# Sums over two chunks of exponentials added beforehand on VectorE, for two head pairs of each later batch

## The reference

```python
# first layer, per batch: 16 heads of 64, 256 tokens, 512 context rows
q = (lat @ Wq);  k, v = split(ctx @ Wkv);  k = apply_rope(k, cos, sin)
attn = clip(q @ k.T * scale, -11, 11)
attn = softmax(attn, axis=-1)
x = x + (attn @ v) @ Wo + bo
# second layer, per token: attention among 16 heads of width 8, then 8 experts
kv = (h @ Wdown + bdown) @ Wup + bup
x = x + out_proj;  x = x + sum_e gate_e * (h2 @ We[e])
```

## Time and profile before

| | |
|---|---|
| time, median of 3 runs | 317.58 us (317.51 to 318.62) |
| the profiled execution's own time | 318.85 us |
| its span, first to last instruction | 317.0 us |
| TensorE busy | 295.0 us (93%) |
| VectorE busy | 241.6 us (76%) |
| GpSimd busy | 208.6 us (66%) |
| ScalarE busy | 164.0 us (52%) |

### The profile page before, as it was taken

One profiled execution on the slowest core, in us unless ns is written; L12 is line 12 of the kernel. 1 busy time (PEld: TensorE's weight loads), 2 busy tenths in 40 slices (PEclk: granted clock), 3 DMA queues, 4 the chain that ended last, 5 costly groups with the idle time before them and its releaser, 6 DMA issues.

```text
span 317.0 us, 6676 instructions
## 1 busy us (share of the span) xinstructions
PE 295.0 (93%) x2514; PEld 206.9 (65%) x2514; DVE 241.6 (76%) x448; ACT 164.0 (52%) x326; POOL 208.6 (66%) x207
## 2 busy tenths in 40 slices
PE   6888999999999999998999999999999999899983
PEld 6776576666668766665777676566786665486651
DVE  2985997675884849899888788977647699687856
ACT  2446456667443735573425555874426468404741
POOL 5445875765572839786645777498927588868764
PEclk9999999999999999999999999999999999999998
DMA  7563412111210111111111112011101100000001
GB/s 207 169 160 90 134 44 68 52 35 46 58 26 9 38 31 35 36 33 33 35 35 33 28 27 50 13 40 37 32 19 33 47 7 2 0 19 0 3 0 33
DMA packets 16319, 14.24 MB, mean 45 GB/s; under 512 B 4832, under 2 KB 11808, under 8 KB 16288
## 3 DMA queue, kind: packets, MB, share of 16 engines
q1 hardware_dynamic: 14992, 13.49, 16.2%
q10 hardware_dynamic: 1296, 0.33, 0.5%
HBM read 4.89 MB, written 0.52 MB: 17 GB/s over the span
## 4 chain that ended last, share of the span: by engine, by line
PE 54%; DVE 20%; issue 7%; POOL 5%; ACT 5%; DMA 4%; SPq 3%; POOLq 0%; ACTq 0%; DVEq 0%
PE pv L631 12%; PE sc L617 10%; PE sums L652 7%; PE side L738 4%; PE pj_k L555 3%; SPq L522 3%; DVE ks L1262 3%; PE side L814 2%; PE pj_k L557 2%; PE pj_k L556 2%; DMA kswap<-ksin 2%; DMA sin_in<-in_L_xattn_sin_dram 2%; DVE ksin L1326 2%; ACT e L926 2%; POOL e L1768 1%
## 5 line engine op out<-in xcount | busy, mean ns | idle before, releaser
L1768 POOL TENSOR_SCALAR e<-e 128x1024 f32<-128x1024 f32 x64 | 71.6, 1118 | 64.2 <-ACT e L926 56.8
L926 ACT ACTIVATE e<-sc 128x1024 f32<-128x1024 f32 x64 | 65.6, 1025 | 31.3 <-PE sc L617 31.2
L617 PEld LDWEIGHTS sc<-qs,ks 64*128 64x128 f32 x768 | 49.6, 185 | 25.9 <-issue 24.0
L617 PE MATMUL sc<-qs,ks 64*128 64x256 f32 x768 | 62.5, 294 | 2.3 <-ACT e L926 2.2
L631 PE MATMUL pv<-e,v 128*64 128x256 f32 x512 | 62.3, 385 | 1.6 <-POOL e L1768 1.1
L1761 POOL TENSOR_TENSOR krot<-kcos,kswap 128x512 f32<-128x512 f32 x32 | 45.7, 1429 | 9.4 <-DMA kswap<-ksin 7.6
L631 PEld LDWEIGHTS pv<-e,v 128*64 128x64 f32 x512 | 34.1, 136 | 24.0 <-issue 6.8
L934 ACT ACTIVATE u<-pv 128x256 f32<-128x256 f32 x32 | 12.4, 386 | 61.6 <-PE pv L631 61.6
L1262 DVE TENSOR_TENSOR ks<-krot,ks 128x512 fp32r<-128x512 f32 x32 | 32.4, 1012 | 0.1
L1326 DVE TENSOR_TENSOR ksin<-pj_k,sinT 128x512 f32<-128x512 f32 x32 | 21.9, 685 | 3.8 <-PE pj_k L557 3.5
L918 ACT ACTIVATE v<-pj_k 128x512 f32<-128x512 f32 x28 | 16.5, 600 | 13.9 <-PE pj_k L557 13.5
(11 more groups left out here) (293 smaller groups left out, 578.1 us busy)
## 6 DMA issues: line engine op xcount, KB each, us to landing
kswap<-ksin SPq DMA_DIRECT2D x126, 64.0 KB, 2.0
ctx_in<-in_ctx_dram SPq DMA_DIRECT2D x4, 256.0 KB, 3.5
prod<-in_L_xattn_Wkv_dram SPq DMA_DIRECT2D x2, 512.0 KB, 6.3
x_in<-in_x_dram SPq DMA_DIRECT2D x1, 512.0 KB, 6.4
prod<-in_L_xattn_Wq_dram SPq DMA_DIRECT2D x1, 512.0 KB, 7.2
wo<-in_L_xattn_Wo_dram SPq DMA_DIRECT2D x1, 512.0 KB, 4.4
fwe<-in_L_ffn_We_dram SPq DMA_DIRECT2D x1, 512.0 KB, 4.4
out_dram<-x_in SPq DMA_DIRECT2D x3, 128.0 KB, 1.8
```

The source lines that it names most:

```text
L617: last = nc.tensor.matmul(sc[:, h, c * NT:(c + 1) * NT], ks[rows, j % 3, k_part, chunk], qs[rows, j % 2, q_part, :], start=(k_part + q_par ...
L926: nc.scalar.activation(e[:, j % 3, :, 2 * half:2 * half + 2, :].rearrange("p h c n -> p h (c n)"), sc[:, :, :], ACT.Exp, scale=SCALE).then ...
L1768: nc.gpsimd.tensor_scalar(a, a, EXP_HIGH, EXP_LOW, ALU.min, ALU.max).then_inc(s_clip, 1)
```

## The change

`chunks_added(j)` holds for the first batch as before, and now for pairs 2 and 3 of each later batch (pairs 10, 11, 18, 19, 26, 27). For these VectorE runs `add_chunks` twice a pair, in the slot after the pair's own (slots 11 and 12, 19 and 20, 27 and 28), right behind `key_lo` and ahead of the "mid" pieces. The results go to `e_added_later`, which lies in the buffer `on`. `sums(11)`, `sums(19)` and `sums(27)` use 8 matmuls in place of 16 (the profile records each as two), and wait for the additions. They move within slots 12, 20 and 28, from ahead of `times_values` to the end of the slot, behind side step "b" and the `values` unit. In the first batch, and for the other pairs, nothing changes.

```diff
+def chunks_added(j):
+    return j < PAIRS or j % PAIRS in (2, 3)
...
+        e_added_later = on.rearrange("p k n -> p (k n)").rearrange("p (j c h n) -> p j c h n", j=2, c=2, h=2)
...
+        def added_of(pair):
+            return e_added if pair < PAIRS else e_added_later
...
 # TensorE, sums(j)
-                if j < PAIRS:
+                if chunks_added(j):
                     n = 2
-                    pe.wait_ge(s_added, 2 * j + 2)
+                    pe.wait_ge(s_added, 2 * sum(chunks_added(i) for i in range(j + 1)))
...
 # TensorE, the loop over slots
-                if 2 <= slot <= NPAIR and slot % 2 == 0:
+                late = slot > PAIRS and chunks_added(slot - 1)
+                if 2 <= slot <= NPAIR and slot % 2 == 0 and not late:
                     sums(slot - 1)
                 if 1 <= slot <= NPAIR:
                     times_values(slot - 1)
...
                 for n in value_units(slot):
                     values(n)
+                if slot % 2 == 0 and late:
+                    sums(slot - 1)
...
 # VectorE, add_chunks(j, half)
-                nc.vector.tensor_tensor(e_added[:, j % 2, half, :, :], e[:, j % 3, :, 2 * half, :],
+                nc.vector.tensor_tensor(added_of(j)[:, j % 2, half, :, :], e[:, j % 3, :, 2 * half, :],
                                         e[:, j % 3, :, 2 * half + 1, :], ALU.add).then_inc(s_added, 1)
...
 # VectorE, the loop over slots
                     key_lo(slot + 1)
+                if slot > PAIRS and chunks_added(slot - 1):
+                    add_chunks(slot - 1, 0)
+                    add_chunks(slot - 1, 1)
                 second_layer(slot, "mid")
```

More of the change, by code:

```diff
@@ L652, in sums @@
                         last = nc.tensor.matmul(sum_bank[32 * g:32 * g + 32, 0:NT], w,
-                                                e_added[:, pair % 2, c, g % 2, :] if j < PAIRS
+                                                added_of(pair)[:, pair % 2, c, g % 2, :] if chunks_added(j)
                                                 else e[:, pair % 3, g % 2, c, :],
```

## The result

The changed kernel takes 322.64 us (median of 4 runs, 321.65 to 324.38) against 317.54 us for the kernel before on the same chip: ratio 1.014, interval 1.0108 to 1.0172. It is slower, by more than the range of the prediction allowed. A later repetition gave 1.0134 (1.0075 to 1.0194), a difference of 3.9 us between the medians where this one has 5.1.

What follows compares the result with a forecast made beforehand. The prediction took TensorE's instruction list, busy 93% of the span, as the bound. Its places summed to -1.4 + 1.9 + 0.5 = +1.0 us on the 317.58 us median: 318.6 us, +0.3%, range 315.4 to 321.4.

Steps and rivals of the forecast that it cites:

- waiting GpSimd work going behind both additions: Slots 11, 19, 27: GpSimd's waiting clip starts only after both VectorE additions, delaying the release by 1.2 us in slots 20, 28.
- The first rival: VectorE and GpSimd swap the shared SBUF access after each addition; sum +3.6 us, 321.2 us, slower; chance 0.27.
- likeliest case: GpSimd waits behind both additions: -1.4 (slot 12), +1.9 (slot 20), +0.5 (slot 28), 318.6 us; chance 0.50.
- The saving: Three calls of `sums` on TensorE go from 1.86 to 1.00 us: 0.86 us each, 2.6 us in all.
- The wait for `recS`: TensorE's 0.93 us wait at the start of slot 17, expected to shrink by 0.54 to about 0.4 us.
- The root: GpSimd's inverse root in slot 19, behind the clip, expected 1.2 us later, moving the release in slot 20 equally.
- the uncovered release: VectorE's bank release for `keyval2`: in slot 20 1.0 us after TensorE's earlier arrival, in slot 28 0.34 us ahead, without push.
- VectorE is never late: Rival: VectorE's idle quarter absorbs the additions in all slots, leaving only -2.6 us, 314.1 to 315.0 us; chance 0.10.
- The access costs nothing: Rival: shared SBUF access delays no GpSimd work here; -1.8 + 0.7 - 0.7 = -1.8, 315.8 us; chance 0.13.

Runs made afterwards that it cites:

- the run with the PSUM operand: Changed kernel with the second operand of the twelve new additions read from PSUM instead of SBUF: 317.61 us, ratio 0.9971 to the kernel before.
- the middle batch alone: Changed kernel with the change kept only for pairs 18 and 19 (slots 19 and 20): 320.73 us, ratio 1.0068 to the kernel before.
- the filled waits: Changed kernel plus matmuls that serve nothing where TensorE would wait, in slots 12, 20 and 28: 322.12 us, ratio 1.0095 to the kernel before.
- the move alone: Changed kernel without the twelve new additions; sums of slots 12, 20, 28 moved but over four chunks: 320.06 us, ratio 1.0051 to the kernel before.
- the early form of all three places: Changed kernel; pairs 10, 18, 26, 19 added in own slots, `sums(19)` at its old place, `query_down` additions before context split: 316.13 us, ratio 0.9922 to kernel before.
- the own-slot version: Changed kernel with additions of pairs 10, 18, 26 made late in their own slots: 318.95 us, ratio 1.0008 to the kernel before.

## Why the prediction was wrong

One mechanism was taken the wrong way round, one term was not in the sum at all, and some smaller ones were mis-sized.

**The step that failed** is "waiting GpSimd work going behind both additions". The first rival holds: the access changes hands after each instruction. What I had named as its sign, an addition of over 0.7 us, is there in five of the six pairs (in slot 11 both), and the run with the PSUM operand shows that it goes away with the second SBUF operand, their number and place unchanged. The prediction even had the clue in hand: it took the 1.32 us of the clip in slot 19 to mean that the clip had stood waiting behind the key split, and then let it begin behind two additions that come only after that split. I had followed one undisturbed pair against two rows beside it that spoke for the rival. It is also the only pair of the first batch whose additions stand back to back; in the other seven the second waits for a clip, which is the 12.1 us of the earlier trace rows. Why that pair, with a rotation waiting since 43.64, kept the access stays open. It is no accident: the pair takes 1.28 us and that rotation 2.34 in all thirteen traces, while the six new pairs went by the order of asking.

**By places**, likeliest case, rival, and measured:

| | likeliest | rival | measured | of it without the clock |
|---|---|---|---|---|
| slot 12, with the wait for `recS` | -1.4 | +0.7 | +0.57 | +0.57 |
| slot 20 | +1.9 | +1.7 | +3.22 | +1.74 |
| slot 28 | +0.5 | +1.2 | +0.93 | +0.93 |
| behind slot 28 | | | -0.23 | -0.23 |
| sum | +1.0 | +3.6 | +4.5 | +3.0 |

For slot 12 the rival's working stands: in slot 11 the additions fell behind the clip with a rotation between them, ksin came 2.3 us late (110.45, against 108.92 less the 0.80 us by which slot 12 starts earlier in this execution; 2.7 foreseen), the second additions ended at 116.63, and TensorE, there at 115.72, waited 1.05 us. That its figure for slot 20 comes so near the 1.74 is partly luck: it pushed GpSimd's root back by 1.04 us, where it was 0.64, and left out what the stop and the move cost.

**The clock** was in no case of mine: +1.48 us in slot 20, on which the middle batch alone and the filled waits agree. Without it the three slots would have given +3.0 and a time of 317.54 + 3.0 = 320.5, inside the range, though by the rival's mechanism; the filled version's ratio, 1.0095, makes 320.6 of the same 317.54. The one timed execution that can't have had the fall took 321.65, just outside.

**The saving** was right: `sums` runs at 1.07 us in two places, against 1.93 for the four-chunk form in the move alone. But the places keep only 0.66 and 0.56 of the 0.86 where nothing waits. I had costed the move of `sums` at its waits alone; it also costs 0.2 us a place, since it breaks up a run of projections.

**The wait for `recS`** was a misread slack. I gave 0.54 of it back; it is 0.91 us in the changed kernel and in the move alone, 0.91 to 0.92 with the PSUM operand, where slot 12 was 0.67 shorter. Two things were wrong. In the changed kernel VectorE has no such lead: `kv` starts at 116.55 us, 8.34 behind the scores of slot 12, where it was 8.40 before. And where it has one, with the PSUM operand (6.52, so 1.9 us ahead), it doesn't keep it: it waits for ScalarE on the way, 0.91 us there. VectorE's timeline shows that wait before and after the change:

```profile
128.23 0.42 DVE L1262 TENSOR_TENSOR qs<-pj_k,qs 128x256 fp32r<-128x256 f32 x1 [0.91 <-ACT qs L909]
```

```profile
127.88 0.42 DVE L1275 TENSOR_TENSOR qs<-pj_k,qs 128x256 fp32r<-128x256 f32 x1 [0.90 <-ACT qs L922]
```

I had counted with idle time of VectorE only at the two ends of the stretch.

**The root** was pushed back by 0.64 us and not 1.2. The stretch of slot 19 runs 0.19 us earlier in this execution (-0.80, +0.57, +0.04); the clip ends at 175.43, the 175.63 of the earlier trace rows less that, since it went ahead of the additions, and only the two root instructions, ending at 177.13 against 176.68 less 0.19, met them. So `keyval2` of slot 20 waited 1.53 and not 2.2 us, and in slot 28 0.18 and not 0.9. That the uncovered release costs a wait even without any push was right: 0.88 us in the move alone, where I had 1.0.

**VectorE is never late** falls with the three waits at `sums`; where it is made true, in the early form of all three places, its price was nearly right (-2.3 of -2.6). **The access costs nothing** falls with the PSUM operand, which makes it true: that kernel is faster, by 0.7 us in the slots and not by 1.8; the difference lies in slot 12, -0.67 and not -1.8, since the wait for `recS` stayed and the move cost 0.2.

## What to carry to other kernels

Before an instruction is moved away from ahead of a waiting one, ask what its time was covering: here 1.86 us of sums hid a release that came 0.9 us late. Put work of VectorE with two SBUF operands where GpSimd has nothing waiting, and early enough that the reader is never there first; the same additions up to a slot earlier, with the release ahead of the split, turned +1.4% into -0.8%, both against the kernel before. Of two readings of a shared resource, take the one that more rows bear out, and put a stall on TensorE into the range as possibly dearer than its length, by up to 1.5 us here.

## What the runs showed of the hardware

A GpSimd instruction that asks before one of two back-to-back VectorE additions with both operands in SBUF goes ahead of it. A pair then took 2.1 to 3.2 us in place of 1.28, five times of six: in slots 19 and 27 a clip was ahead of the first addition, in slots 12 and 28 of the second, and in slot 11 a clip and a rotation were ahead of one each. Order of asking isn't the whole rule: the one pair of the earlier trace rows kept the access with a rotation waiting, in all thirteen traces. With one operand in PSUM the same twelve additions took 672 to 684 ns.

TensorE's granted clock fell to 1.2 GHz behind waits of 1.53 and 0.53 us, in the midst of an otherwise busy stretch, and slot 20 took 1.5 us more than with the clock up. It fell again behind waits of 1.56 and 0.41 us, and behind one of 2.04, there for 0.7 us more (12.41 against 11.70), and in the own-slot version behind 0.90 and 1.05. Waits like the first two, 1.54 and 0.51 us in the kernel with the middle batch alone, left it at 2.4 GHz. So the length of the waits does not decide alone; what else does, these runs don't tell.

Behind a stop of 0.88 us the steps around it took 0.26 us beyond the wait (slot 20 of the move alone, one case), and a change from projections to sums and back cost 0.2 us.
